# Second weights of the experts loaded from ScalarE's DMA queue, the first ones from SyncE's

## The chip, the cores and the metric

The kernel is one program on one core of one Trainium2 chip. The core has five engines with instruction streams of their own: TensorE (PE, with its weight load PEld), VectorE (DVE), ScalarE (ACT), GpSimd (POOL) and SyncE (SP). They meet through semaphores: an instruction can wait for a semaphore to reach a value, and raises one when it is done. A load or store between memory (HBM) and the on-chip buffer is issued by an engine's instruction stream into a DMA queue, and carried out by 16 DMA engines. The metric is the time of one execution in device microseconds (us); lower is better.

## The reference, cut to what matters

The program computes two layers; only the last part of the second one is touched here, the experts behind a gate. There are 64 experts, B is 4 images.

```python
t = t + _L1_attn_ref(_ln_t(t), Wq, Wk, Wv)            # causal attention, 4 x 4096 tokens of 128
t = t + _L1_ffn_ref(_ln_t(t), gate_w, gate_b, weight1, weight2)

def _L1_ffn_ref(x, gate_w, gate_b, weight1, weight2):  # E, H, O, K = 64, 512, 128, 8
    probs = softmax(einsum('bsd,ed->bse', x, gate_w) + gate_b, axis=1)
    vals, idx = top_k(probs.transpose(0, 2, 1), K)     # the 8 best tokens of each expert
    pooled = einsum('bked,bke->bed', gathered, topv)
    h = gelu(einsum('ebd,edh->ebh', [pooled, 1], weight1))   # weight1: 64 x 129 x 512
    out = einsum('ebh,eho->ebo', [h, 1], weight2)            # weight2: 64 x 513 x 128
    outputs = zeros.at[token].add(out * topv)
```

Each expert sees only four pooled rows (one for each image), but its two weight matrices of 128 x 512 numbers each have to come from memory: 16.8 MB of first weights and 16.8 MB of second ones.

## The kernel before, in words

Layer 0 (Fourier convolutions) and the attention of layer 1 fill the first 1885 us and are the same in both kernels. What follows has four parts.

1. After the attention, VectorE finishes the row statistics of the tokens.
2. The gate. In 16 chunks the tokens are normalized (`norm_chunk`, half of each chunk by VectorE on line 848, half by ScalarE on line 675), transposed by TensorE (line 496), copied out of PSUM (line 872 and 689), and multiplied by the gate's weights (line 487); VectorE takes the logits out (line 853). Then come exponentials, the choice of the eight best tokens, the transposed gate values (TensorE line 506, copies on lines 892 and 698) and the pooling matmuls (line 512).
3. The experts, in NG = 16 groups of EG = 4. The weights of a group are one megabyte of first weights, `W1B`, and one of second weights, `W2B`; both lie in the tile V, in four slots, so group g uses slot g mod 4. TensorE's loop over steps s runs `hidden(s)` (line 523, waits for the weights of group s), `turn_hidden(s-1)` (line 531), `result(s-2)` (line 540, raises `e2_mm`) and `turn_result(s-3)` (line 548). Between them stand copies on ScalarE (line 704), the bias on VectorE (line 905), the GELU on ScalarE (line 710) and two copies on VectorE (lines 913 and 917). Beside it VectorE normalizes the tokens (line 928).
4. The last matmuls (line 569), whose results VectorE adds to the tokens (line 941), and the stores (line 347).

SyncE issues the weight loads in `sync_l1`. Those of groups 0 to 2 go out once the attention's last matmul is done (`pv_mm`), those of group 3 once the gate has given up its part of V (`gate_ready`), and those of group g from 4 on once `result(g-4)` has freed their slot: `e2_mm` at g - 3. Since `result(g-4)` stands in TensorE's step g - 2, at most two groups are on their way at a time. Both transfers of a group raise the same semaphore, `ew_in` of the slot, and `hidden(g)` waits for both of them:

```python
pe.wait_ge(sem(f"ew_in{g % 4}"), 32 * (g // 4 + 1))
```

No order is searched by a planner here: every engine's order is that in which the code is written.

Of the kernel before, what the change touches and what calls it, by code (L numbers as in the profile page):

```python
# [33 lines left out]
EX, HID, TOPK = 64, 512, 8  # L34
EG = 4
# [101 lines left out]
def conv_attn_hybrid(nc, io, out):  # L137
    with ExitStack() as ctx:
# [5 lines left out]
        def sem(name):  # L144
            if name not in sems:
                sems[name] = ctx.enter_context(nc.semaphore(name))
            return sems[name]
# [14 lines left out]
        cst, o = {}, 0  # L162
# [123 lines left out]
        NU = UB * B  # L286
# [34 lines left out]
        W2B = VG[:, :, 1, :].rearrange("p c (e k o) -> p c e k o", e=EG, k=4)  # L321
# [6 lines left out]
        NG = EX // EG  # L328

        def sync_l1(sp):  # L330
            sp.wait_ge(sem("l1_start"), 1)
            sp.dma_start(B1T, io["L1_ffn_weight1"][:, D, :].rearrange("e (p k) -> p e k", k=4)).then_inc(sem("b1_in"), 16)
            sp.wait_ge(sem("pv_mm"), NU)
            for g in range(NG):
                if g == 3:
                    sp.wait_ge(sem("gate_ready"), 2)
                if g >= 4:
                    sp.wait_ge(sem("e2_mm"), g - 3)
                e = slice(EG * g, EG * g + EG)
                sp.dma_start(W1B[:, g % 4], io["L1_ffn_weight1"][e, 0:D, :].rearrange("e d h -> d e h")).then_inc(sem(f"ew_in{g % 4}"), 16)  # L340
                sp.dma_start(W2B[:, g % 4].rearrange("p e k o -> p e (k o)"),
                             io["L1_ffn_weight2"][e, 0:HID, :].rearrange("e (p k) o -> p e (k o)", k=4)).then_inc(sem(f"ew_in{g % 4}"), 16)
            for s in range(8):
                sp.wait_ge(sem("fin_ready"), 4 * s + 4)
                for b in range(2 * (s // 4), 2 * (s // 4) + 2):
                    i = T * b + 8 * (s % 4)
                    sp.dma_start(out_nat[:, i:i + 8, :], U[:, i:i + 8, :]).then_inc(sem("out_done"), 16)
            sp.wait_ge(sem("out_done"), 16 * 4 * B)
# [262 lines left out]
        def scalar_l1(act):  # L611
# [60 lines left out]
            def norm_chunk(c):  # L672
                i = NT * (2 * (c // 8) + 1) + 4 * (c % 8)
                for j in range(i, i + 4):
                    ins = act.activation(U[:, j, :], U[:, j, :], ACT.Identity, scale=tkr[:, j:j + 1], bias=tkn[:, j:j + 1])
                ins.then_inc(sem("xn_ready1"), 1)

            def gate_exp(q):
                act.wait_ge(sem("gm_ready"), q + 1)
                act.activation(LG[q], LG[q], ACT.Exp, bias=gmx[:, q, 0:1], accum_out=gmx[:, q, 1:2]).then_inc(sem("gexp_ready"), 1)  # L680

            norm_chunk(0)
            for c in range(16):
                if c + 1 < 16:
# [8 lines left out]
            for q in range(2):  # L693
                for g in range(1, 8, 2):
                    act.wait_ge(sem("g_mm"), 32 + 8 * q + g + 1)
                    if q:
                        act.wait_ge(sem("pool_mm"), 1)
                    act.activation(AF[1][:, 512 * g:512 * g + 512], PS[:, g % 4, :], ACT.Copy).then_inc(sem("g_ev1"), 1)
            for s in range(NG + 1):
                if s < NG:  # L700
                    act.wait_ge(sem("e1_mm"), s + 1)
                    if s >= 2:
                        act.wait_ge(sem("ht_mm"), s - 1)
                    act.activation(HP[s % 2], PS[:, s % 2, :], ACT.Copy).then_inc(sem("hp_ready"), 1)
                if s >= 1:
                    g = s - 1
                    act.wait_ge(sem("h_ev"), g + 1)
                    if g >= 2:
                        act.wait_ge(sem("e2_mm"), g - 1)
                    act.activation(HG[g % 2][:, 0:64], HB[:, g % 2, :], ACT.Gelu).then_inc(sem("hg_ready"), 1)  # L710

        def fold_weights(dve, later):


            dve.wait_ge(sem("l1w_in"), 16 * 8)
            later(dve.tensor_copy(w0, WN3[:, :, 0]))
            for i in range(3):
                ins = dve.tensor_scalar(WN3[:, i, :], WN3[:, i, :], w0[:, i:i + 1], None, ALU.subtract)
            ins.then_inc(sem("fold_ready"), 1)
            dve.memset(pb, LIFT * float(np.log(2.0)))  # L720
            dve.wait_ge(sem("wt_mm"), 1)
            later(dve.tensor_scalar(AHL[0], PS[:, 1, 0:128], AUP, None, ALU.mult))
            dve.scalar_tensor_tensor(AHL[1], PS[:, 1, 0:128], AUP, AHL[0], ALU.mult, ALU.subtract)
            dve.tensor_copy(WV[:, 0:128], PS[:, 1, 128:256])
            dve.memset(WV[:, 129:130], 0.0)
            dve.tensor_scalar(WV[:, 128:129], ident[:, 0:1], 1.0 / 32.0, None, ALU.mult)
            dve.tensor_copy(gwT, PS[:, 1, 384:384 + EX])
            dve.tensor_copy(identh, ident)
            dve.tensor_copy(ident16, ident)
            dve.tensor_copy(mask16, cst["mask"]).then_inc(sem("wt_ready"), 1)  # L730
# [266 lines left out]
        def _(sp):  # L997
# [72 lines left out]
            for k in range(16):  # L1070
                if k >= 3:
                    sp.wait_ge(sem("ax_ready"), k - 2)
                sp.dma_start(AF[1][:, 1024 * (k % 3):1024 * (k % 3 + 1)].rearrange("p (i w) -> p i w", w=W),
                             x_nat[:, 8 * k:8 * k + 8, :]).then_inc(sem(f"xr_in{k % 3}"), 16)

            sync_l1(sp)


# [248 lines left out]
        def _(act):  # L1327
# [108 lines left out]
            for g in range(NIM):  # L1436
                if g % 4 < 3:
                    for i in range(4 * g, 4 * g + 4):
                        ins = act.activation(Vn[:, i, :], Vn[:, i, :], ACT.Identity, scale=WS[:, 3, i:i + 1], bias=WS[:, 7, i:i + 1])
                    ins.then_inc(sem("mn_act"), 1)  # L1440
            scalar_l1(act)


# [395 lines left out]
```

## Time and profile before

| what | us |
|---|---|
| median of 3 runs (2133.42 to 2134.83) | 2134.35 |
| profiled execution, its own time | 2136.38 |
| profiled execution, its span | 2134.5 |
| PE busy | 1755.9 (82%) |
| DVE busy | 1604.7 (75%) |
| ACT busy | 1071.7 (50%) |
| POOL busy | 356.2 (17%) |
| 32 weight loads of 1024 KB, median from issue to landing | 7.7 |

The span is the time from the first to the last instruction of the profiled execution; its own time is 1.9 us longer, for what lies around it. Shares are averages over stages that have different limits: in the last 250 us the DMA engines are busy in a few stretches alone, and these are looked at one by one. Times of rows are us from the start of the span unless marked ns. SPq is SyncE's instruction stream issuing a transfer; the time given there is that of the issuing instruction, not of the transfer.

### The profile page before, as it was taken

The numbers are of one execution on the slowest core, as the hardware profiler recorded it, in microseconds if no ns is written. First come the engines' busy times: TensorE is split into PE (matmuls) and PEld (weight loads), VectorE is DVE, ScalarE is ACT, GpSimd is POOL, SyncE is SP. The second block draws the span as 40 slices with busy tenths as digits, with TensorE's granted clock in tenths as the row PEclk, the third lists the DMA queues.
The fourth block names the chain that finished last, engine by engine and source line by source line (L and its number), as shares of the span: only waits on it lengthen the run. The fifth ranks groups of instructions, "written<-read, shape, count | busy, mean of one in ns | idle before, by whom it ended". The sixth has DMA issues, their size and how long they took to land.

```text
span 2134.5 us, 31119 instructions
## 1 busy us (share of the span) xinstructions
PE 1755.9 (82%) x11614; PEld 1100.8 (52%) x11614; DVE 1604.7 (75%) x2908; ACT 1071.7 (50%) x1656; POOL 356.2 (17%) x540
## 2 busy tenths in 40 slices
PE   8675556599799987059999999998999999975767
PEld 8631111199789987025444454454544544444625
DVE  4489999936876678959886788778887888668445
ACT  4394000023445244646777677766777666774110
POOL 0000000000063034725210350006110211100000
PEclk9876887799899998569999999999999999987979
DMA  6551768300000032000000000000000000030496
GB/s 166 203 135 48 173 156 191 85 1 1 1 2 1 1 96 69 0 3 1 1 1 1 1 1 1 1 1 1 1 1 1 1 1 1 1 119 1 149 322 200
DMA packets 95251, 114.19 MB, mean 53 GB/s; under 512 B 16128, under 2 KB 68736, under 8 KB 94560
## 3 DMA queue, kind: packets, MB, share of 16 engines
q1 hardware_dynamic: 95104, 112.20, 18.6%
q8 instruction: 96, 1.57, 0.3%
q14 instruction: 51, 0.42, 0.1%
HBM read 99.74 MB, written 12.44 MB: 53 GB/s over the span
## 4 chain that ended last, share of the span: by engine, by line
PE 63%; DVE 23%; issue 6%; ACT 3%; DMA 3%; POOL 1%; SPq 1%; POOLq 0%; DVEq 0%; ACTq 0%
DVE U L951 7%; PE PS L427 5%; PE PS L429 5%; PE PS L428 5%; PE PS L446 5%; PE PS L447 5%; PE PS L448 5%; PE PS L1115 4%; PE PS L1188 4%; PE PS L1197 4%; PE PS L409 4%; DVE U L963 3%; DMA V<-in_L_ffn_weight 3%; PE PS L1298 3%; DVE ST L1666 1%
## 5 line engine op out<-in xcount | busy, mean ns | idle before, releaser
L796 DVE TENSOR_TENSOR DB<-Z 128x1024 f16<-128x1024 f32 (+2 forms) x288 | 336.9, 1170 | 128.8 <-ACT Z L633 76.4
L630 ACT ACTIVATE Z<-PS,MI 128x1024 f32<-128x1024 f32 (+2 forms) x288 | 300.7, 1044 | 229.4 <-PE PS L429 191.9
L782 DVE TENSOR_REDUCE MI<-PS 128x1 f32<-128x512 f32 (+2 forms) x576 | 359.5, 640 | 54.7 <-PE PS L409 35.5
L633 ACT ACTIVATE Z<-PS,MI 128x1024 f16<-128x1024 f32 (+2 forms) x288 | 298.9, 1038 | 0.0
L951 DVE TENSOR_TENSOR U<-A,U 128x4224 f32<-128x4224 f32 x48 | 215.1, 4553 | 0.1
L1285 PE MATMUL PS<-U 128*32 128x352 f32 x1152 | 131.7, 606 | 93.1 <-DVE U L951 93.1
L598 POOL TENSOR_SCALAR Z<-Z,MI 128x128 f32<-128x128 f32 x128 | 86.1, 683 | 719.2 <-DVE MI L811 719.2
L1086 POOL TENSOR_SCALAR U<-U,MI 128x128 f32<-128x128 f32 x128 | 56.0, 456 | 603.6 <-DVE V L1723 603.6
L1285 PEld LDWEIGHTS PS<-U 128*32 128x32 f32 x1152 | 39.8, 131 | 184.0 <-DVE U L951 118.9
L1372 ACT ACTIVATE Z<-PS 128x352 f32<-128x352 f32 x6 | 2.8, 464 | 225.1 <-PE PS L1285 225.1
L446 PE MATMUL PS<-Z,A 128*128 128x512 f16 (+3 forms) x288 | 104.3, 362 | 3.9 <-ACT CST L641 3.6
L446 PE MATMUL PS<-Z,V 128*128 128x512 f16 (+3 forms) x288 | 104.0, 361 | 2.9 <-ACT CST L641 2.8
L1188 PE MATMUL PS<-CST,A 128*66 128x128 f32 x768 | 105.2, 281 | 0.5 <-DVE A L1662 0.5
L1197 PE MATMUL PS<-CST,DB 66*128 66x128 f32 x768 | 103.6, 278 | 1.9 <-ACT DB L1404 1.4
L427 PE MATMUL PS<-V 128*128 128x512 f16 (+3 forms) x288 | 104.7, 363 | 0.0
L427 PE MATMUL PS<-A,V 128*128 128x512 f16 (+3 forms) x288 | 104.6, 363 | 0.0
L429 PE MATMUL PS<-A,V 128*128 128x512 f16 (+3 forms) x288 | 104.5, 363 | 0.0
L428 PE MATMUL PS<-A,V 128*128 128x512 f16 (+3 forms) x288 | 104.5, 363 | 0.0
L428 PE MATMUL PS<-V 128*128 128x512 f16 (+3 forms) x288 | 104.4, 363 | 0.0
L429 PE MATMUL PS<-V 128*128 128x512 f16 (+3 forms) x288 | 104.3, 362 | 0.0
L447 PE MATMUL PS<-DB,A 128*128 128x512 f16 (+3 forms) x288 | 104.1, 362 | 0.0
L447 PE MATMUL PS<-DB,V 128*128 128x512 f16 (+3 forms) x288 | 104.0, 361 | 0.0
(400 smaller groups left out, 3815.3 us busy)
## 6 DMA issues: line engine op xcount, KB each, us to landing
V<-in_L_ffn_weight SPq DMA_DIRECT2D x32, 1024.0 KB, 7.7
U<-e_planes SPq DMA_DIRECT2D x192, 132.0 KB, 5.0
A<-x_planes SPq DMA_DIRECT2D x24, 528.0 KB, 10.3
U<-in_x SPq DMA_DIRECT2D x16, 512.0 KB, 3.7
V<-in_x SPq DMA_DIRECT2D x4, 2048.0 KB, 13.8
Z<-in_x SPq DMA_DIRECT2D x16, 512.0 KB, 3.9
out<-U SPq DMA_DIRECT2D x16, 512.0 KB, 5.4
x_planes<-Z SPq DMA_DIRECT2D x2, 1056.0 KB, 8.0
```

The lines of the kernel that those rows point to most:

```text
L427: pe.matmul(o, kh[:, ks], qh[:, qs], start=True, stop=False)
L428: pe.matmul(o, kh[:, ks], ql[:, qs], start=False, stop=False)
L429: mm = pe.matmul(o, kl[:, ks], qh[:, qs], start=False, stop=k < 4 * g)
L446: pe.matmul(o, xh[:, k, :], ph, start=k == 0, stop=False)
L447: pe.matmul(o, xh[:, k, :], pl, start=False, stop=False)
L630: act.activation(EX32[u % 2][:, 0:w], s, ACT.Exp, scale=SCALE / (QUP * KUP), bias=pb).then_inc(sem("ex_ev"), 1)
L633: act.activation(EHI[u % 3][:, 0:w], s, ACT.Exp, scale=SCALE / (QUP * KUP), bias=pb).then_inc(sem("hi_ev"), 1)
L782: dve.tensor_reduce(bm[:, g % 2, t, k:k + 1], PS[:, 4 + chunk_no[c] % 2, 0:w], AX.X, ALU.max).then_inc(sem("ch_ev"), 1)
L796: dve.tensor_tensor(ELO[u % 3][:, 0:w], EX32[u % 2][:, 0:w], EHI[u % 3][:, 0:w], ALU.subtract).then_inc(sem("lo_ev"), 1)
L951: eng.tensor_tensor(YB[:, k % 2].rearrange("p b k m -> p b (k m)"), XR[:, r % 2].rearrange("p b k m -> p b (k m)"), EB[:, k % NEB].rearran ...
L1188: mm = pe.matmul(PS[0:66, 4 + k % 2, 128 * j:128 * j + 128], A_modes[:, :, 4 * k + j], cst["ih"], start=True, stop=True)
L1197: mm = pe.matmul(PS[:, 6 + k % 2, 128 * j:128 * j + 128], DB[0:66, k % 3, 128 * j:128 * j + 128], cst["iw"][0:66, :], start=True, stop=True)
```

## The change

SyncE's loop over the groups issues only the first weights. The second weights are issued by ScalarE's instruction stream, on its own DMA queue, by a new helper `load_second(g)` with the same waits. It is called in three places: for groups 0 to 2 ahead of `norm_chunk(0)`, for group 3 behind the copies of the transposed gate values, and for group s + 2 at the end of step s of ScalarE's loop over the groups.

```diff
-                sp.dma_start(W2B[:, g % 4].rearrange("p e k o -> p e (k o)"),
-                             io["L1_ffn_weight2"][e, 0:HID, :].rearrange("e (p k) o -> p e (k o)", k=4)).then_inc(sem(f"ew_in{g % 4}"), 16)
...
+            def load_second(g):
+                if g == 3:
+                    act.wait_ge(sem("gate_ready"), 2)
+                if g >= 4:
+                    act.wait_ge(sem("e2_mm"), g - 3)
+                act.dma_start(W2B[:, g % 4].rearrange("p e k o -> p e (k o)"),
+                              io["L1_ffn_weight2"][EG * g:EG * g + EG, 0:HID, :].rearrange("e (p k) o -> p e (k o)", k=4)
+                              ).then_inc(sem(f"ew_in{g % 4}"), 16)
+
+            act.wait_ge(sem("pv_mm"), NU)
+            for g in range(3):
+                load_second(g)
             norm_chunk(0)
...
+            load_second(3)
             for s in range(NG + 1):
                 if s < NG:
                     act.wait_ge(sem("e1_mm"), s + 1)
...
                     act.activation(HG[g % 2][:, 0:64], HB[:, g % 2, :], ACT.Gelu).then_inc(sem("hg_ready"), 1)
+                if 4 <= s + 2 < NG:
+                    load_second(s + 2)
```

The first place is on ScalarE where the gate begins. The line numbers of the changed kernel are two lower than before for what stands behind the loop of SyncE (675 becomes 673) and ten or eleven higher behind the helper. Before:

```order
L614 ACTIVATE MI<-MI 128x128 [waits var_ready]
L675 ACTIVATE U<-U,Z 128x128 [waits coef_ready]
L675 ACTIVATE U<-U,Z 128x128 x7
L689 ACTIVATE DB<-PS 128x512 [waits g_mm]
L675 ACTIVATE U<-U,Z 128x128 x4
```

And now:

```order
L612 ACTIVATE MI<-MI 128x128 [waits var_ready]
L685 DMA V<-in_L_ffn_weight 128x4x512 [waits pv_mm,coef_ready]
L685 DMA V<-in_L_ffn_weight 128x4x512 x2
L673 ACTIVATE U<-U,Z 128x128 x8
L699 ACTIVATE DB<-PS 128x512 [waits g_mm]
L673 ACTIVATE U<-U,Z 128x128 x4
```

Three issues (second weights of groups 0 to 2) stand ahead of the first two chunks that ScalarE normalizes, and behind the same wait for the coefficients.

The second place is ScalarE's loop over the groups, here steps 2 to 4. Before:

```order
L704 ACTIVATE DB<-PS 128x512 [waits ht_mm,e1_mm]
L710 ACTIVATE MI<-MI 128x64 [waits h_ev]
L704 ACTIVATE DB<-PS 128x512 [waits ht_mm,e1_mm]
L710 ACTIVATE MI<-MI 128x64 [waits e2_mm,h_ev]
L704 ACTIVATE DB<-PS 128x512 [waits ht_mm,e1_mm]
```

And now, with the issue of group 3 ahead of the loop:

```order
L708 ACTIVATE Z<-PS 128x512 [waits pool_mm,g_mm] x4
L685 DMA V<-in_L_ffn_weight 128x4x512 [waits gate_ready]
L715 ACTIVATE DB<-PS 128x512 [waits e1_mm] x2
L721 ACT_TABLE_LOAD
L721 ACTIVATE MI<-MI 128x64 [waits h_ev]
L715 ACTIVATE DB<-PS 128x512 [waits ht_mm,e1_mm]
L721 ACTIVATE MI<-MI 128x64 [waits h_ev]
L685 DMA V<-in_L_ffn_weight 128x4x512 [waits e2_mm]
L715 ACTIVATE DB<-PS 128x512 [waits ht_mm,e1_mm]
L721 ACTIVATE MI<-MI 128x64 [waits e2_mm,h_ev]
L685 DMA V<-in_L_ffn_weight 128x4x512 [waits e2_mm]
```

Each issue of groups 4 to 15 stands between the GELU of one group (line 721) and the copy of the hidden values of a later one (line 715).

## Rows read from the trace of the kernel before

**Rows 1.** The page's shares of the chain that ended last, by engine
```profile
PE 63%; DVE 23%; issue 6%; ACT 3%; DMA 3%; POOL 1%; SPq 1%; POOLq 0%; DVEq 0%; ACTq 0%
```

**Rows 2.** Chain of waits, 2000 to 2097: start us, us, what
```profile
2007.88 0.37 SPq L340
2008.29 8.48 DMA V<-in_L_ffn_weight
...
2025.43 11.12 DMA V<-in_L_ffn_weight
...
2041.06 7.46 DMA V<-in_L_ffn_weight
...
2078.55 10.39 DMA V<-in_L_ffn_weight
```

**Rows 3.** Groups by line, 2007.9 to 2089: busy us, mean ns | idle before, releaser
```profile
L523 PE MATMUL PS<-V,ST 128*32 128x512 f32 x100 | 19.5, 859 | 32.7 <-DMA V<-in_L_ffn_weight 32.6
```

**Rows 4.** Stretches: us; busy of PE, PEld, DVE, ACT, POOL; PEclk; DMA share; GB/s
```profile
2007.90:2089.00 81.10, 48.41 (x544) 23.92 (x536) 33.80 (x139) 10.26 (x24) 0.00 (x0) 0.77 0.87 312
...
2036.60:2048.60 12.00, 8.79 (x94) 4.00 (x97) 5.19 (x22) 1.71 (x4) 0.00 (x0) 0.74 0.99 350
```

**Rows 5.** Timeline of SyncE's queue, the first six loads: start us, us, what
```profile
1885.44 0.37 SPq L340 DMA_DIRECT2D V<-in_L_ffn_weight  x1
1885.85 0.51 SPq L341 DMA_DIRECT2D V<-in_L_ffn_weight  x1
1886.40 0.51 SPq L340 DMA_DIRECT2D V<-in_L_ffn_weight  x1
1886.95 0.80 SPq L341 DMA_DIRECT2D V<-in_L_ffn_weight  x1
1887.80 2.08 SPq L340 DMA_DIRECT2D V<-in_L_ffn_weight  x1
1889.92 2.82 SPq L341 DMA_DIRECT2D V<-in_L_ffn_weight  x1
```

**Rows 6.** Timeline, beginning of the gate, all engines; idle before in brackets
```profile
1897.65 3.19 ACT L675 ACTIVATE U<-U,Z 128x128 f32<-128x128 f32 x8 [1.47 <-DVE MI L842]
...
1898.70 3.67 PE L496 MATMUL PS<-CST,U 128*128 128x128 f32 x16 [10.63 <-DVE U L848]
...
1902.30 1.35 PE L487 MATMUL PS<-DB,Z 128*64 128x512 f32 x4
...
1903.70 0.75 DVE L853 TENSOR_SCALAR_CACHE_REDUCE A<-PS,Z 128x512 f32<-128x512 f32 x1 [1.46 <-PE PS L487]
...
1911.33 0.60 ACT L689 ACTIVATE ST<-PS 128x512 f32<-128x512 f32 x1 [0.17 <-PE PS L496]
```

**Rows 7.** Timeline, experts, steps 3 and 4, then step 5's beginning
```profile
2010.39 0.26 ACT L710 ACTIVATE MI<-MI 128x64 f32<-128x64 f32 x1 [1.05 <-PE PS L540]
2010.42 0.37 SPq L340 DMA_DIRECT2D V<-in_L_ffn_weight  x1
...
2020.10 0.26 ACT L710 ACTIVATE MI<-MI 128x64 f32<-128x64 f32 x1 [0.69 <-DVE MI L905]
...
2021.72 0.37 SPq L340 DMA_DIRECT2D V<-in_L_ffn_weight  x1
...
2022.11 1.16 PE L523 MATMUL PS<-V,ST 128*32 128x512 f32 x8
...
2023.35 0.60 ACT L704 ACTIVATE DB<-PS 128x512 f32<-128x512 f32 x1 [2.99 <-PE PS L523]
```

**Rows 8.** Timeline: last copy of the gate, and `hidden(3)`
```profile
1986.92 0.60 ACT L698 ACTIVATE Z<-PS 128x512 f32<-128x512 f32 x1 [0.28 <-PE PS L506]
...
2007.63 1.04 PE L523 MATMUL PS<-V,ST 128*32 128x512 f32 x8
```

**Rows 9.** Timeline: VectorE's normalization before and during loads
```profile
2003.05 2.14 DVE L928 TENSOR_SCALAR U<-U,MI 128x128 f32<-128x128 f32 x8
...
2025.35 2.13 DVE L928 TENSOR_SCALAR U<-U,MI 128x128 f32<-128x128 f32 x8
```

## The prediction

> **What bounds the kernel now.** I read the page's shares of the chain first, then the chain of waits in the last 250 us, where alone anything changes, then the stretches of that part, and last the timelines around each place at which an issue is taken away or put in. Over the whole kernel TensorE is 63% of the chain and DMA only 3% [rows 1], so a change to loads can reach a small part. But that part is dense: between 2008 and 2089 us the chain runs through six waits for expert weights, one for every two groups, from 7.46 to 11.12 us in length; the first three and the last are in [rows 2]. In that stretch of 81.1 us TensorE's line 523, `hidden`, sits idle for 32.6 us behind the loads [rows 3]. So the expert stage is bound by its loads, and the reader's question has to be: by their bandwidth, or by when they are issued? The stretches answer with both. Over the 81.1 us the DMA engines are busy 0.87 of the time at 312 GB/s; in the best pair of groups, 12.0 us long, 0.99 of the time at 350 GB/s [rows 4]. All that is one queue's work. One queue fills the engines whenever it has something to do, and the missing 13% are the moments in which the next pair has not been issued yet: `e2_mm` of group g-4 comes only behind `hidden(g-2)` in TensorE's order, thus behind the landing of the group two before.
>
> **The change part by part.** I call the three places A, B, C.
>
> A, the beginning of the gate. Before, the six loads of groups 0 to 2 went out of SyncE's stream between 1885.44 and 1892.74 us, beside the statistics, and nobody waited [rows 5]. Now three of them stand on ScalarE ahead of its first two normalizations. They wait for the coefficients as those did, so they start when line 675 started, 1897.65 [rows 6]. The trace holds no DMA issue by ScalarE, so its price is bounded by SyncE's. Three in a row on an empty queue: from 1885.44 to the start of the fourth at 1886.95 is 1.51 us. Three on a queue that is filled already: the fourth to sixth took 0.80 + 2.08 + 2.82 = 5.70 us [rows 5]. ScalarE's queue is empty and the first weights have landed by then, so I take 1.51, the row whose situation is the same; 5.70 is the upper end and, if an issue costs ScalarE's engine nothing, 0 the lower one.
>
> What queues behind it: the eight normalizations (3.19 us), the first copy, and through these TensorE. ScalarE's first chunk is done 3.19 / 2 = 1.60 and 1.51 us after 1897.65, at 1900.76, and the second at 1902.35. A group of four transposes is 3.67 / 4 = 0.92 us. TensorE has the first of VectorE's at 1899.62, then waits for ScalarE's to 1900.76 and is done with it at 1901.68, does VectorE's second to 1902.60 and ScalarE's second to 1903.52; only then comes the first logits matmul, which started at 1902.30 [rows 6]. That is 1.2 us later; 0.3 of the 1.51 is swallowed, as TensorE was behind anyway. VectorE waited 1.46 us for that matmul, so its line 853 moves by the same 1.2. From there VectorE sets the pace and had no idle time to give; ScalarE catches up by itself, since from 1911.33 on it waits for TensorE in each chunk [rows 6]. So A = +1.2 us, between 0 and 5.70 - 0.3 = +5.4.
>
> B, group 3. Its second weights were issued together with the first ones and are now issued behind ScalarE's last copy of the gate, which ends at 1987.52. `hidden(3)` runs at 2007.63 [rows 8], 20.1 us later. The longest wait of the chain from an issue to a landing, 11.12 us [rows 2], would still end 9 us before that. B = 0; were that cover gone, each microsecond of lateness would count once.
>
> C, the loop. Three questions. Does ScalarE issue late? Its issue waits for `e2_mm` as SyncE's did and stands behind a GELU. That GELU ran at 2020.10 to 2020.36 and SyncE was released at 2021.72: ScalarE stands ready 1.4 us earlier. At one of the 12 issues it is the other way round, by 2010.65 - 2010.42 = 0.2 us [rows 7], which the transfer of the first weights covers. Does the issue hold up ScalarE? Behind it stands the copy of line 704, for the hidden values. In the tightest case seen, SyncE issued at 2021.72 and line 704 started at 2023.35 [rows 7]; an issue of 0.4 to 0.5 us ends by 2022.3. Free, with 1.1 us of cover; were it gone, every microsecond of it would delay `turn_hidden` and the next `e2_mm`. Does the second queue move bytes faster, or worse? The second weights' issue comes 0.41 us earlier, as SyncE no longer issues the first ones before it, but they need the engines only once these have moved a megabyte, which at 350 GB/s takes 3.0 us. With 0.99 of the time busy on one queue [rows 4], the nearest row says that there is nothing to win in a full stretch, so I take C = 0. The bounds are wide. Below: if two queues made each of the six pairs as short as the best one, 81.1 - 6 x 12.0 = 9.1 us would go. Above: if the two queues served the later group's first weights ahead of the earlier group's second ones, the earlier group would land later by one megabyte, 3.0 us, in each of six pairs: +18 us.
>
> The stretch of 12.0 us at 350 GB/s is the measured ceiling of one queue here. A rule of the Trainium skill (DMA: Bandwidth & Descriptors, "Issuing engines are not separate DMA queues") speaks against this change: transfers started from different engines run on the same 16 DMA engines and interleave, and starting them from two engines saves only the time of issuing. By the rule C is 0; no run here shows two queues at once, and the share of 0.99 with one queue agrees with it. By the row alone up to 9.1 us could still go, in the pairs that were not full.
>
> Compute beside the loads is not slowed by them: eight normalizations on VectorE took 2.14 us with no load under way and 2.13 us beside one [rows 9]. So moving three loads from the statistics into the gate costs nothing more.
>
> Sum: A 1.2 + B 0 + C 0 = +1.2 us. Against the profiled execution's own 2136.38 us (span 2134.5 and 1.9 around it) that gives 2137.6; that execution was 2.0 us above the median of the runs, 2134.35, so on the median the forecast is 2135.5 us.
>
> **The rivals.** R1, faster: two queues close the seams between transfers and the ramp after an empty queue. For it: a pair takes 81.1 / 6 = 13.5 us in the mean where one took 12.0, and the engines were idle 13% of the stretch [rows 4]. Against it: that idle time is mostly from late issues, which the change leaves as late as they were. Price: four fifths of the bound, -7.3, and A's +1.2: 2128.3 us. It needs over 5.5 us from C to leave the band of no change.
>
> R2, slower: sharing between the queues. As soon as group g+1 is issued while g is under way, SyncE's queue holds first weights of g and g+1, ScalarE's the second ones. If the engines serve them evenly, both halves of g end together and as early as before; if they favour SyncE's, g's second half ends after g+1's first. At half of the +18 it costs 9, in all 2144.6 us; it decides from 0.5 us a pair. For it: nothing in the trace orders one queue against another. Against it: both halves are equally large and issued within 0.4 us. The Trainium skill says (same page, "Queues, rings and completion order") that each DMA engine takes turns between its queues packet by packet; by that rule the halves end together and R2 gives 0; no run here shows it.
>
> R3, slower, ScalarE's issue is dear: at 5.70 us for three the gate begins 5.4 us late and the time is 2139.8. It leaves the band from about 4.6 us for three. The same price in the loop, 1.9 us an issue, would begin to eat the cover of 1.1 us in the tight steps.
>
> That the change does nothing of what it says (no load really beside another) is part of the forecast: both queues then still share the same engines.
>
> **How the numbers follow.** Forecast 0.73, R1 0.12, R2 0.09, R3 0.06. A change of under 0.2%, 4.3 us, is about what a measurement of this kernel can tell from none. Inside the forecast A and C may come out anywhere from -3 to +4, so all of it lies in the band. Faster is R1 with a bit of the forecast's edge, 0.13; slower is R2 and R3 together, 0.15, less the part of R3 that stays in the band, 0.14; the same 0.73. The range goes down to 2128, to hold R1's price, and up to 2141, to hold R3; it leaves out R2 and the tails.
>
> **What would show it.** A: on ScalarE three issues ahead of its first normalization, some 1.5 us in all, the first logits matmul 1.2 us later after VectorE's first coefficient, and ScalarE level with VectorE again after some ten chunks. B: group 3's second weights landed long before its `hidden`. C: six waits for weights on the chain again, together as long as before within 3 us; ScalarE's issues of 0.4 to 0.5 us within 0.4 us of SyncE's; a DMA share near 0.87 over the stretch, 81 us long. I would be wrong if that stretch were shorter than 77 us (R1), or the first group of each pair landed more than 0.5 us later after its issue (R2), or one issue on ScalarE took over 1.5 us (R3).

## The result and the profile after

| | before | changed |
|---|---|---|
| median of the runs beside the prediction | 2133.52 (7 runs, 2130.95 to 2134.83) | 2140.74 (7 runs, 2138.00 to 2143.01) |
| ratio | | 1.0032, 95% interval 1.0019 to 1.0046 |
| the same kernel beside the last experiments | 2136.70 (29 runs, 2129.79 to 2142.00) | 2139.36 (11 runs, 2136.56 to 2143.58) |
| ratio | | 1.0011, 95% interval 1.0000 to 1.0022 |
| profiled execution, span | 2134.5 | 2138.9 |

The changed kernel is slower, by 7 us in the first measurement and by 2.7 in the second; the two intervals share only 1.0019 to 1.0022. The two profiled executions differ by 4.4 us in span: +3.9 us in the expert loop, -1.3 us in the gate, and +1.8 us that was there already at the first weight load (1887.28 us for 1885.44), ahead of everything that the change touches. The other 2.9 us of the first measurement is in no stage: the profiled execution of the kernel before was that much above the median of its seven runs. Both of these are scatter between executions. So I compare stages, not spans.

The page's lines on the queues and the issues, where all loads were on SyncE's queue before:

```profile
q1 hardware_dynamic: 86656, 95.42, 16.4%
q10 hardware_dynamic: 8448, 16.78, 2.2%
...
V<-in_L_ffn_weight SPq DMA_DIRECT2D x16, 1024.0 KB, 8.1
V<-in_L_ffn_weight ACTq DMA_DIRECT2D x16, 1024.0 KB, 9.8
```

ScalarE's loads are queue q10, 16.78 MB as intended; the median landing of a megabyte is later on both queues than the 7.7 us of before.

**The gate.** The gate is measured from VectorE's first normalization to `hidden(0)`. The timeline of its beginning, which answers to [rows 6]:

```profile
1899.48 1.53 ACTq L685 DMA_DIRECT2D V<-in_L_ffn_weight  x3
...
1901.06 3.19 ACT L673 ACTIVATE U<-U,Z 128x128 f32<-128x128 f32 x8 [3.04 <-issue]
...
1902.76 2.82 PE L494 MATMUL PS<-CST,U 128*128 128x128 f32 x12 [1.11 <-ACT U L673]
...
1905.52 1.98 PE L485 MATMUL PS<-DB,Z 128*64 128x512 f32 x4
...
1907.54 0.75 DVE L866 TENSOR_SCALAR_CACHE_REDUCE A<-PS,Z 128x512 f32<-128x512 f32 x1 [2.08 <-PE PS L485]
```

Three issues hold ScalarE for 1.53 us, the 1.51 of SyncE's. From VectorE's first normalization (1899.37 here, 1897.53 before) to the first logits (line 866, 853 before: VectorE's lines stand thirteen lower down in the changed kernel) it now takes 8.17 us instead of 6.17, so +2.0: 1.4 from the later start of the matmul, and 0.6 because that matmul took 1.98 us instead of 1.35. Yet from the same normalization to `hidden(0)` it takes 103.67 us, against 104.99 before: 1.3 us less. So 3.3 us were given back, at three places. The first is the rest of the chunks, from the first logits taken to the last, before and then changed:

```profile
1903.70:1942.25 38.55, 32.47 (x172) 16.08 (x172) 33.22 (x100) 32.49 (x69) 0.00 (x0) 0.91 0.00 1
...
1907.54:1945.03 37.49, 31.34 (x172) 15.40 (x172) 33.11 (x100) 32.19 (x67) 0.00 (x0) 0.95 0.06 23
```

TensorE was busy 1.1 us less, at a granted clock of 0.95 instead of 0.91, and the stretch is 1.1 us shorter. The other 2.2 us came back in the transposes of the gate values (line 506 before, 504 after), 0.7 us in the first set of 32 and 1.5 us in the second. By line, and then for the second set by stretch, before first:

```profile
L506 PE MATMUL PS<-CST,A x64: 272/421/476, 1958.8 to 1986.6; 128*128 128x128 f32 x64
...
1981.60:1987.00 5.40, 5.23 (x32) 5.00 (x32) 2.59 (x4) 1.87 (x4) 0.00 (x0) 0.70 0.82 268
```

The same of the changed kernel:

```profile
L504 PE MATMUL PS<-CST,A x64: 272/273/475, 1961.6 to 1987.1; 128*128 128x128 f32 x64
...
1982.10:1987.30 5.20, 4.00 (x36) 3.73 (x35) 3.90 (x6) 1.79 (x3) 0.00 (x0) 1.00 0.55 157
```

The columns of the line are ns min/median/max. The median transpose took 273 ns instead of 421, and TensorE's granted clock in that stretch was 1.00 (2.4 GHz) instead of 0.70. The gate took 103.67, 103.83 and 103.75 us in the three executions with the issues in it, and 104.7 to 105.1 us in eight of the nine without them. I take the shift in time for the cause of the other clock, but that is not shown: the ninth (e2) had no issue in the gate, and there the clock was 1.00 in the chunks, the second set was as fast as in the changed kernel, and the gate took 100.31 us.

**The expert loop.** I measure it from the end of the first `result` to the start of `hidden(15)`: 81.16 us before, 85.08 after. A pair of groups is one even group and the odd one behind it: 4 and 5, 6 and 7, and so on. The chain through the changed loop, which answers to [rows 2]:

```profile
2008.40 9.19 DMA V<-in_L_ffn_weight
...
2022.55 9.52 DMA V<-in_L_ffn_weight
2032.11 1.93 PE PS L521 x8
2034.05 1.06 PE PS L529 x4
2035.11 1.91 PE PS L538 x32
2037.04 8.94 DMA V<-in_L_ffn_weight
...
2050.95 9.65 DMA V<-in_L_ffn_weight
...
2068.13 11.59 DMA V<-in_L_ffn_weight
...
2082.58 10.79 DMA V<-in_L_ffn_weight
```

The two waits of the chain before that [rows 2] leaves out:

```profile
2052.09 9.63 DMA V<-in_L_ffn_weight
...
2064.99 10.29 DMA V<-in_L_ffn_weight
```

Before, the chain went through the second group of a pair in five waits of six, all but that at 2008.29; its bytes stood in the queue behind the first's. Now four of the six waits, up to 2050.95, are for the first group of a pair, and only the last two for a second one. From a first group the chain goes on through `hidden`, `turn_hidden` and `result` to the next pair's first issue.

Here is the lost time. From the release of a pair's first group (the end of the `result` that frees its slot) to its `hidden` it took 9.55 us in the mean of six, against 8.65 before; below this is called the wait for the first of a pair. It adds 5.4 us in the six pairs. The work from there to the next pair's release adds 0.7 us in five, and the last step, from `hidden(14)` to `hidden(15)`, gives back 2.2 us (4.63 for 6.80): +3.9 in all. The second groups landed no later, 14.4 us after the pair's first issue before and 14.2 us after it now, in the mean of six. In the second pair the two groups had landed 8.1 and 14.8 us after the pair's first issue before, and 9.5 and 14.2 us after it now.

A first group is also the dearer one to stand on the chain, because of what TensorE's clock is behind it. The three stages from a landing to the next release, after a first group and after a second one, both in the changed kernel:

```profile
2017.63:2022.53 4.90, 4.90 (x45) 2.43 (x45) 0.23 (x1) 0.85 (x2) 0.00 (x0) 0.50 0.76 280
2079.76:2082.56 2.80, 2.80 (x45) 1.64 (x45) 2.10 (x9) 0.85 (x2) 0.00 (x0) 1.00 0.78 191
```

The same work took 4.90 us at a granted clock of 0.50 (1.2 GHz) and 2.80 us at 1.00 (2.4 GHz). TensorE had stood idle for 6.5 us before the first of them and for 0.3 us before the second. Before the change it was the same behind the first group (4.86 us at 0.50), but the chain passed there only once. Along the chain TensorE's work adds up to 20.7 us before and 25.0 us now, and what lies between it, from a release to the next `hidden`, to 60.5 and 60.1 us. The stretch of the whole loop and the groups by waits, where [rows 4] had 0.87 and 312 GB/s and [rows 3] 32.6 us:

```profile
2008.40:2093.40 85.00, 46.97 (x540) 23.54 (x532) 32.07 (x134) 10.26 (x24) 0.00 (x0) 0.74 0.84 297
...
PE PS L521 <- DMA V<-in_L_ffn_weight: 38.0, 8, 6.8
```

TensorE waits 38.0 us for weights. The DMA engines are no slower when full: 2011.4 to 2017.6, ahead of the first landing, is one stretch of sharing, by queue (packets, MB, share):

```profile
DMA packets 1203, 2.40 MB, mean 387 GB/s; under 512 B 32, under 2 KB 32, under 8 KB 1203
## 3 DMA queue, kind: packets, MB, share of 16 engines
q10 hardware_dynamic: 598, 1.19, 52.2%
q1 hardware_dynamic: 605, 1.21, 51.7%
```

The same stretch of the kernel before, with one queue:

```profile
DMA packets 1209, 2.40 MB, mean 387 GB/s; under 512 B 39, under 2 KB 39, under 8 KB 1209
```

387 GB/s is what one queue reached too, and it is shared evenly, 605 packets to 598. Each megabyte is 512 packets, and counted in the order of its queue, these divide the 0.9 us. Two megabytes of the loads issued from a pair's first issue on had moved after 7.31 us before and 7.40 us now, so the start is not slower. The last packet of the first group itself came after 7.44 us before and 7.88 us now: that half is order, since 0.19 MB of the next group had moved ahead of it, against 0.03 MB before. From that packet to the landing it took 1.1 us before and 1.6 us now. That other half stays open: the records do not say which of the 16 engines moved a packet, so the last one to finish can't be followed.

### The profile page after: what moved, and what is told of

Its sections match the earlier page's. It is cut to its first block, busy times and chain, and to the rows that moved or that the text cites. A ratio compares the mean times of both kernels' runs of the same rounds, so it can differ in the third digit from the quotient of the medians.

```text
span 2138.9 us, 31120 instructions
## 1 busy us (share of the span) xinstructions
PE 1750.3 (82%) x11614; PEld 1096.4 (51%) x11614; DVE 1604.1 (75%) x2908; ACT 1071.7 (50%) x1656; POOL 357.3 (17%) x540
## 3 DMA queue, kind: packets, MB, share of 16 engines
q10 hardware_dynamic: 8448, 16.78, 2.2%
## 4 chain that ended last, share of the span: by engine, by line
PE 62%; DVE 23%; issue 6%; ACT 4%; DMA 3%; POOL 1%; ACTq 0%; POOLq 0%; DVEq 0%; SPq 0%
DVE U L964 7%; PE PS L425 5%; PE PS L427 5%; PE PS L426 5%; PE PS L444 5%; PE PS L445 5%; PE PS L446 5%; PE PS L1128 4%; PE PS L1201 4%; PE PS L1210 4%; PE PS L407 4%; DVE U L976 3%; DMA V<-in_L_ffn_weight 3%; PE PS L1311 3%; DVE ST L1679 1%
## 5 line engine op out<-in xcount | busy, mean ns | idle before, releaser
L425 PE MATMUL PS<-A,V 128*128 128x512 f16 (+3 forms) x288 | 104.7, 363 | 0.0
```

The source lines that it names most:

```text
L425: pe.matmul(o, kh[:, ks], qh[:, qs], start=True, stop=False)
```

## The experiments

Stages of the profiled executions, and the times:

| kernel | gate, us | loop, us | wait for the first of a pair, us | ratio to before (95%) |
|---|---|---|---|---|
| before | 104.99 | 81.16 | 8.65 | |
| changed | 103.67 | 85.08 | 9.55 | 1.0032 (1.0019 to 1.0046) |
| e1 gate part | 103.83 | 81.21 | 8.84 | 0.9995 (0.9985 to 1.0006) |
| e2 loop part | 100.31 | 85.41 | 9.62 | 1.0015 (1.0003 to 1.0027) |
| e3 five to three | 104.70 | 84.25 | 8.97 | 1.0009 (1.0000 to 1.0018) |
| e4 three to five | 104.86 | 83.52 | 9.15 | 1.0013 (1.0000 to 1.0026) |
| e7 groups in turn | 104.73 | 85.22 | 9.58 | 1.0024 (1.0014 to 1.0033) |
| e8 changed again | 103.75 | 85.03 | 9.54 | 1.0011 (1.0000 to 1.0022) |
| e9 swapped | 104.96 | 81.27 | 8.74 | 0.9999 (0.9988 to 1.0010) |
| e10 ScalarE first | 105.04 | 85.21 | 9.43 | 1.0016 (1.0003 to 1.0028) |
| e5 early first | 105.13 | 66.06 | | 0.9929 (0.9915 to 0.9943) |
| e6 early, two queues | 105.04 | 74.17 | | 0.9965 (0.9953 to 0.9978) |

The loop is the steadier witness: two executions of the changed kernel gave 85.08 and 85.03 us, and the two with one queue 81.16 and 81.21. Each of the others was profiled once.

Edits are shown against the changed kernel, that of e5 against the kernel before. In e2 to e4, e6, e7, e9 and e10 the loads of groups 0 to 3 all stay on SyncE.

**e1, the gate part alone**

```diff
+                if g >= 4:
+                    sp.dma_start(W2B[:, g % 4] ...   # groups 4 to 15 stay on SyncE
...
-                if 4 <= s + 2 < NG:
-                    load_second(s + 2)
```

> Only the second weights of groups 0 to 3 go through ScalarE's queue; those of groups 4 to 15 stay on SyncE's. Theory T1 (the loss lies in the expert loop: two queues that share evenly let the first weights of group g+1 pass the second ones of group g, 0.9 us a pair): the loop stretch of 79 us is as before, the first of a pair lands 8.6 us after its issue, and what is left of the loss is the beginning of the gate, whose first logits are taken 2.0 us later after the coefficients in the profile after; since most of that was regained by the end of the gate, 0 to +2 us against before. Rival T3 (the three issues ahead of the gate carry the loss): +5 to +7 us.

The loop was as before and the time 0.05% lower, with an interval around zero. T3 is out: the three issues ahead of the gate do not carry the loss.

**e2, the loop part alone**

```diff
+                if g < 4:
+                    sp.dma_start(W2B[:, g % 4] ...   # groups 0 to 3 on SyncE
...
-            act.wait_ge(sem("pv_mm"), NU)
-            for g in range(3):
-                load_second(g)
...
-            load_second(3)
```

> Only the second weights of groups 4 to 15 go through ScalarE's queue; all of groups 0 to 3 stay on SyncE's. T1 (sharing in the loop): the first of a pair lands 9.5 us after its issue instead of 8.6, six pairs, +5 us against before. T3 (the gate carries the loss): within 1 us of before.

The loop took 85.41 us, +4.2, and the time was +0.15% (3 us): the loss is here. The gate, which this edit leaves as it was before, took only 100.31 us in the profiled execution, at a granted clock of 1.00 in the chunks.

**e3, five to three**

```diff
+                sp.dma_start(W2B[:, g % 4, 0:1] ...        # one expert's second weights on SyncE
...
-                act.dma_start(W2B[:, g % 4] ...
+                act.dma_start(W2B[:, g % 4, 1:4] ...
```

> As e2_loop_part, but the bytes of a group of 4 to 15 are split 5 to 3: SyncE loads the first weights and the second weights of one expert (1.31 MB), ScalarE the second weights of three experts (0.79 MB). T1: ScalarE's bytes begin some 1 us after SyncE's, which at 390 GB/s is a lead of 0.39 MB; with this split both halves of a group end together (1.22 to 0.83 would be exact), the first of a pair lands 8.6 us after its issue again, and the time is within 1.5 us of before. T2 (two queues cost the engines throughput, whatever the split): +5 us as in e2_loop_part.

The wait for the first of a pair was 8.97 us, two thirds of the way back, but the loop still took 84.25 us. That speaks for T1 against T2 in direction, and not in size: the time, +0.09%, tells neither from the other. A group moves in three transfers here and in e4 instead of two, so it is not the split alone that differs.

**e4, three to five**

```diff
-                sp.dma_start(W1B[:, g % 4] ...
+                sp.dma_start(W1B[:, g % 4, 0:3] ...        # three experts' first weights on SyncE
...
+                act.dma_start(W1B[:, g % 4, 3:4] ...
                 act.dma_start(W2B[:, g % 4] ...
```

> As e2_loop_part, but split 3 to 5: SyncE loads the first weights of three experts (0.79 MB), ScalarE the first weights of the fourth and all second ones (1.31 MB). T1: SyncE's lead leaves ScalarE 0.9 MB behind when SyncE has finished its part of the group; at half the rate this takes up to 2.3 us longer than alone, where the equal split lost 1.0: the first of a pair lands 10 to 11 us after its issue and the time is 8 to 14 us above before. T2 (throughput): +5 us as in e2_loop_part.

A miss: the wait for the first of a pair was 9.15 us, and the loop took 83.52 us, less than with equal halves. The packet records show why more bytes on ScalarE's queue did not cost more. T1 needs SyncE's first weights of the next group to pass; but these, though issued before SyncE's queue had run empty, began only 2.9 to 4.0 us after their issue. In the second pair they were issued at 2027.19 and began at 2030.90, and meanwhile ScalarE's queue had the engines to itself (2028.9 to 2030.9):

```profile
q10 hardware_dynamic: 389, 0.80, 104.1%
q1 hardware_dynamic: 1, 0.00, 0.3%
```

**e7, whole groups in turn**

```diff
+                if g >= 4 and g % 2:
+                    continue                          # odd groups: both halves on ScalarE
...
+                if g % 2 == 0:
+                    return
+                act.dma_start(W1B[:, g % 4] ...
                 act.dma_start(W2B[:, g % 4] ...
```

> The bytes of groups 4 to 15 again go half through each queue, but whole groups in turn: even groups on SyncE's, odd ones on ScalarE's. T1 (even sharing lets the later group take engines from the earlier one): when the odd group's bytes start, some 3.3 us behind the even one's, 0.9 to 1.0 MB of the even one are still to come and move at half the rate, so it lands 2.4 us later than alone, in six pairs: +8 to +14 us against before, two or three times the loss of e2_loop_part. T2 (two queues cost throughput, whoever holds what): +3 to +5 us, as e2_loop_part. T4 (ScalarE's queue starts about 1 us later than SyncE's, and only that lateness counts): 3 pairs' worth or less, under +3 us.

+0.24%, 5 us, is outside what T1 and T4 said and in the range of T2. But T2 can't be it: with both queues at work the engines moved the same 387 GB/s as with one. The two queues did not share as T1 has it either. ScalarE's first issue of group 7, and the queues in the stretch around it:

```profile
2025.65 0.37 ACTq L691 DMA_DIRECT2D V<-in_L_ffn_weight  x1
...
q1 hardware_dynamic: 1043, 2.08, 79.2%
q10 hardware_dynamic: 48, 0.10, 3.3%
```

Between 2022.6 and 2030.3 us SyncE's queue moved 2.08 MB and ScalarE's 0.10, though ScalarE had issued at 2025.65: its bytes began 4.0 us after the issue, when SyncE's were nearly done, and the wait for the first of this pair was only 8.7 us. In the first pair it was 11.4 us. There ScalarE's bytes began 3.7 us after their issue, with more of SyncE's still to come, and once begun they took most of the engines (2013.5 to 2017.0):

```profile
q10 hardware_dynamic: 529, 1.07, 80.3%
q1 hardware_dynamic: 177, 0.33, 24.7%
```

SyncE's second weights, running beside them, took 6.3 us for a megabyte. So the even sharing of queues holds here only where both are given work at the same moment. A queue that is issued while the other has work before it starts late, and after that need not take turns evenly. T1 as I had put it is wrong in this; its price of a passed group shows in three pairs of six (11.4, 9.8 and 9.9 us).

**e8, the changed kernel again** (nothing edited)

> The changed kernel once more, beside the two below and the kernel before on the same chip. If the loop carries the loss (e2_loop_part +0.15%, e1_gate_part -0.05%), it lies 3 to 7 us above before and its first groups of a pair land 9.5 us after their issue. If the gate part costs as much again on top, +7 us or more.

+0.11% (interval 0 to 0.22%) is just below the range expected, though the loop reproduced to 0.05 us. Loop +3.9 and gate -1.2 make +2.7 us, and 0.11% is 2.3. I take the first measurement's +0.32% to be that plus scatter between sessions, which I can't show.

**e9, queues swapped**

```diff
-                sp.dma_start(W1B[:, g % 4] ...
+                sp.dma_start(W2B[:, g % 4] ...
...
-                act.dma_start(W2B[:, g % 4] ...
+                act.dma_start(W1B[:, g % 4] ...
```

> As e2_loop_part with the queues swapped for groups 4 to 15: first weights through ScalarE's, second ones through SyncE's, both still issued at the same moment. If ScalarE's queue itself starts later whenever both are given work at once (T4), now the first weights land last in each group, by 1.3 us, and the time is that of e2_loop_part, +3 to +5 us. If the kind of transfer sets who lags (first weights ahead, whatever the queue), the second weights land last again.

ScalarE's half again ended last, by 0.9 us from last packet to last packet in the mean of the six first groups, as in the changed kernel; so it is the queue and not the kind of transfer that lags. But the stretch was that of before:

```profile
2010.62:2091.89 81.27, 50.14 (x540) 24.30 (x533) 33.78 (x139) 10.29 (x25) 0.00 (x0) 0.75 0.87 311
```

Two queues, the same lag, and no loss in the loop. The times can't confirm it: the ratio is 0.9999, but the median, 2139.18 us, lies nearly as far above before as that of e8 (2139.36). The loop of this one profiled execution fits what the chain shows in the others. The wait for the first of a pair is 8.74 us, and the chain runs through second groups in five waits of six, as before. In the third and fourth pair the second group was issued 6.6 and 6.8 us after the first, where the changed kernel has 3 us, so it had little or nothing to pass. The start was not quicker (two megabytes after 7.51 us), and the first group's last packet came after 7.93 us, as in the changed kernel; the difference lies between that packet and the landing (0.7 us for 1.6). Why it is smaller with the first weights on ScalarE's queue stays open.

**e10, ScalarE's issue first**

```diff
-                    sp.wait_ge(sem("e2_mm"), g - 3)
+                    sp.wait_ge(sem("rb_ready"), g - 3)
```

> As e2_loop_part, but SyncE's issue for a slot waits for VectorE's copy of the result (rb_ready) instead of for the result itself, and so comes 0.3 to 0.45 us after ScalarE's. If the queue that is issued first takes the lead, now ScalarE's second weights start and land first, and the loss stays at +3 to +6 us, since by T1 it is the lead of either queue that lets the next group's bytes pass. If both queues then start together, the two halves of a group land within 0.5 us of each other and the time is within 1.5 us of before, plus up to 1 us for the six later issues.

The first issues of the loop:

```profile
2007.84 0.43 ACTq L688 DMA_DIRECT2D V<-in_L_ffn_weight  x1
2008.16 18.33 SPq L340 DMA_DIRECT2D V<-in_L_ffn_weight  x4
```

The second row merges four issues. 0.32 us of head start turned the order round: now ScalarE's half of the first group ended 1.5 to 2.5 us ahead of SyncE's. The loop took 85.21 us, +0.16% in time, as the first case had it. A lead of ScalarE's twice as long cost what SyncE's costs in the changed kernel, and in e9 SyncE's lead cost nothing in the loop, so the lead alone does not set the loss.

**e5, first weights issued early, one queue**

```diff
+                if g >= 4:
+                    sp.wait_ge(sem("e1_mm"), g - 3)    # ahead of the first weights
...
+                if g >= 4:
+                    sp.wait_ge(sem("e2_mm"), g - 3)    # ahead of the second ones alone
```

> One queue, as before, but SyncE issues the first weights of group g as soon as hidden(g-4) has read the slot (e1_mm at g - 3) instead of waiting for result(g-4); the second weights still wait for result(g-4). If the stage is bound by late issues and not by bandwidth, three groups' first weights fill the time in which the DMA engines had nothing to do (0.11 to 0.13 of 81 us), and the stage shrinks by 8 to 14 us. If the engines were the bound, within 2 us of before.

```profile
2010.04:2076.10 66.06, 42.49 (x540) 21.76 (x532) 34.43 (x141) 10.29 (x25) 0.00 (x0) 0.87 1.00 368
```

The DMA engines are now busy all the time at 368 GB/s, the loop is 15.1 us shorter, one more than the 14 expected, and the kernel ran in 2122.51 us (median of 6) against 2137.40 before, 0.71% faster. This is the version that beats both kernels. The gap that the change left alone was worth four times what it cost.

**e6, the same with two queues**

```diff
-                    sp.wait_ge(sem("e2_mm"), g - 3)
+                    sp.wait_ge(sem("e1_mm"), g - 3)    # SyncE: first weights; ScalarE: second ones
```

> As e5_early_first, but the second weights of groups 4 to 15 are issued by ScalarE on its own queue, so the first weights no longer stand behind them and run up to four groups ahead. Late issue is gone as in e5_early_first: 8 to 14 us under before. By T1 the second weights then share with first weights that are not urgent, which takes back 1 to 4 us of it; if sharing does no harm it is as fast as e5_early_first or faster.

```profile
2009.56:2083.73 74.17, 44.62 (x541) 22.85 (x533) 34.15 (x141) 10.31 (x25) 0.00 (x0) 0.82 0.93 328
```

2128.23 us, 5.7 us above e5, and the loop 8.1 us longer: more than the 1 to 4 us expected. e5 and e6 differ in the second queue and in what that lets happen, first weights running ahead of their turn, so this is the strongest sign that here order in one queue is worth more than a second one. It does not part the two.

## Why the prediction was right or wrong

The forecast was +1.2 us, 2135.5 us, and no measurable change. The time, 2140.74 us, lay within the range, 5 us above the point and 0.3 us below the upper end, which had been put there to hold R3. A change of +0.32% is more than the 0.2% that the prediction called measurable, the +0.11% of the second measurement less. That the sum came near is partly luck: A was to cost 1.2 us and gained 1.3, C was to cost nothing and cost 3.9. By its steps:

- **What bounds the loop**: right. It was late issue, not bandwidth, that kept the stage at 81 us: e5 brought the share from 0.87 to 1.00 and took 15.1 us out.
- **A, the gate**: the issues cost 1.53 us where 1.51 was said. The logits moved by 2.0 us, not 1.2: the term left out that the matmul behind the wait would itself run at a lower clock (1.98 for 1.35 us). The stage as a whole became 1.2 to 1.3 us shorter, which no rival had. "From there VectorE sets the pace and had no idle time to give" was a wrong reading: in the chunks before, from 1903.70 to 1942.25 us, VectorE stood idle for 6.6 us behind line 487, and a TensorE busy 1.1 us less made them 1.1 us shorter; 2.2 us more came back in the transposes, at a higher clock. The prediction had no term for the clock. ScalarE was level again, as said: from 1915.16 us on its copies waited for TensorE.
- **B, group 3**: right. Its second weights had landed 5.1 us after their issue at 1987.45, 15.6 us ahead of `hidden(3)`.
- **C, the loop**: this step failed. Its first two questions were answered rightly: ScalarE stood ready (its GELU ended at 2021.18 and the issue went out at 2022.55) and the issue cost it nothing. The third was not. "The nearest row says that there is nothing to win in a full stretch, so I take C = 0" took full engines to mean that nothing could be lost. +3.9 us were, while the engines moved the same 387 GB/s: the first group of each pair came 0.9 us later, and the chain turned to pass through the first groups, behind which TensorE's stages take 4.1 to 4.9 us instead of 2.8.
- **R2, slower by sharing**, named the place and was priced at 9 us, between 0 and 18; it measured 3.9. Its case against it (halves issued within 0.4 us end together) was wrong, since the half issued at the same moment on ScalarE's queue had its last packet 0.9 us later and landed 1.7 us later. The Trainium skill's rule there (DMA: Bandwidth & Descriptors, "Queues, rings and completion order"), turns between the queues packet by packet, agrees with the 605 and 598 packets of the stretch from 2011.4 to 2017.6, but not with the 529 and 177 of e7, if both queues had work for every engine there, which the trace does not show; and even with equal turns R2 was not 0.
- The Trainium skill's rule that two issuing engines save only the time of issuing (same page, "Issuing engines are not separate DMA queues") would make C 0; measured in the loop, it was a loss of 4.2 us in e2 and 0.1 us in e9.
- **R1 and R3** fell: nothing got faster in the loop, and an issue on ScalarE took 0.38 to 0.53 us.

What is shown: the loss lies in the loop (e1, e2), in the wait for the first group of a pair (9.5 to 9.6 for 8.65 to 8.84 us), with the engines moving as much as before when both queues are at work. That it comes from the queues' order is argued from the packet records, which give it half of the 0.9 us, and from e10, e5 and e6. The other half is open, e4 and e7 do not fit the simple form of it, and e9 is explained only in part. How much of the 3.9 us would be left if TensorE's clock behind a first group were not 0.50, no run shows.

## What to carry to other kernels

When a stage waits for loads and the DMA engines are not always full, look at which semaphore releases each load before adding a queue: half of a buffer may be free long before the other half, and issuing it then was worth 15 us where the second queue cost 4. A buffer that needs two transfers is ready when the later one lands, so both halves and the next buffer's belong in one queue in the order of need, unless a trace shows that two queues keep that order. Follow the chain by single waits: a change that moves no more and no fewer bytes can still move the chain to a place where another engine is slower. Where a kernel's runs scatter by 0.3%, compare the stage in the profile of several kernels that share it.

## What the runs showed of the hardware

- Two queues issued at the same moment, each with one megabyte in rows of 2 KB, shared packets evenly (605 and 598), but in the changed kernel ScalarE's began 1.0 to 1.6 us after SyncE's and ended 0.5 to 1.3 us after it (six first groups). 0.32 us of head start turned the order round (e10).
- A queue issued while the other had up to two megabytes before it moved nothing for 2.2 to 4.1 us (e7), and then took 529 of 706 packets in 3.5 us.
- One megabyte load held ScalarE's instruction stream for 0.38 to 0.53 us, like SyncE's (0.37 to 0.52 us on a queue that was not yet filled).
- `hidden`, `turn_hidden` and `result` of a group took 4.9 us at a granted clock of 0.50 and 2.8 us at 1.00; 0.50 was granted behind an idle stretch of 6.5 us.
- TensorE's granted clock in a late stage changed with small shifts of an early one: a delay of 2 us early in the gate went with a clock of 1.00 instead of 0.70 in 32 transposes 75 us later, and with a gate 1.2 us shorter, in three executions of three. It is not the only way there: e2 met the fast transposes without the delay.
